# A convolution-and-attention kernel on one core: the first pass hands an eighth of its taps to GpSimd and keeps sums in PSUM, the last pass reorders ScalarE and VectorE steps and is written out without a loop

## What is computed

```
# layer 0: grouped 3x3 convolution with stride 2 (2 channels in, 1 out, 256 groups), gates, upsampling
xd  = conv(x, w_down, stride 2, padding 1, 256 groups)     # 8 x 256 x 64 x 64: 18 taps for each output
labels = kmeans(xd[0]);  gate = sigmoid(gaussian_mixture(means of xd by label))
y   = bilinear_up_x2(repeat(gate * xd + xd, 2) * w_up) + x
# layer 1: linear attention over the 64 lowest cosine frequencies of y
xp  = y @ P   (P: 16384 positions x 64 frequencies);  q, k, v from xp;  out = y + gamma * (...)
```

## Time and profile before

| | us |
|---|---|
| median of three runs | 3655.98 |
| the profiled execution: its own time | 3661.4 |
| the profiled execution: its span | 3659.6 |
| busy in the span: TensorE / VectorE / ScalarE / GpSimd | 3128.9 / 2957.6 / 1880.3 / 637.2 |
| granted TensorE clock, mean | 0.935 of full |

### The profile page before, as it was taken

One profiled execution on the slowest core, in us unless ns is written; L12 is line 12 of the kernel. 1 busy time (PEld: TensorE's weight loads), 2 busy tenths in 40 slices (PEclk: granted clock), 3 DMA queues, 4 the chain that ended last, 5 costly groups with the idle time before them and its releaser, 6 DMA issues. The chain is left out here.

```text
span 3659.6 us, 66212 instructions
## 1 busy us (share of the span) xinstructions
PE 3128.9 (85%) x23398; PEld 2253.8 (62%) x23398; DVE 2957.6 (81%) x3454; ACT 1880.3 (51%) x4327; POOL 637.2 (17%) x325
## 2 busy tenths in 40 slices
PE   7998999999899958995867888889788888888876
PEld 3554545455454526652446877878687787878776
DVE  5999999999999982204556979888897988979877
ACT  4554555555455524241316565655656566565654
POOL 0000000000000000000003333333333333333333
PEclk9999999999999979597978999999999999999999
DMA  6665566556655525252035988988888898888997
GB/s 266 256 248 212 219 257 255 222 212 251 257 233 212 238 114 204 110 217 65 0 132 212 338 331 333 351 317 337 327 326 333 328 347 331 335 326 329 345 346 287
DMA packets 190940, 947.58 MB, mean 259 GB/s; under 512 B 13505, under 2 KB 13633, under 8 KB 170626
## 3 DMA queue, kind: packets, MB, share of 16 engines
q1 hardware_dynamic: 181378, 909.48, 64.3%
q0 software_dynamic: 9216, 33.56, 2.3%
HBM read 638.90 MB, written 301.99 MB: 257 GB/s over the span
## 5 line engine op out<-in xcount | busy, mean ns | idle before, releaser
L190 DVE SCALAR_TENSOR_TENSOR first_acc<-first_x,first_wd,first_acc 128x1024 f32<-128x1024 f32 (+1 forms) x1088 | 1297.9, 1272 | 58.0 <-ACT first_acc L215 45.2
L1290 PE MATMUL second_o<-second_right,second_left 128*128 128x128 f32 x8192 | 1101.0, 285 | 175.2 <-POOL second_left L1074 98.7
L1290 PEld LDWEIGHTS second_o<-second_right,second_left 128*128 128x128 f32 x8192 | 1016.8, 199 | 229.7 <-issue 217.9
L1534 DVE SCALAR_TENSOR_TENSOR second_x<-second_o,second_shift,second_x 128x512 f32<-128x512 f32 x1024 | 732.9, 737 | 233.1 <-PE second_o L1290 231.5
L1074 POOL TENSOR_TENSOR second_left<-second_mid_copy,second_coef_rep 64x1024 f32<-64x1024 f32 x256 | 602.5, 2353 | 1684.5 <-ACT second_mid_copy L1397 1677.4
L219 ACT ACTIVATE first_xT<-first_tp 128x512 f32<-128x512 f32 x1024 | 609.3, 598 | 536.1 <-PE first_tp L245 535.6
L245 PE MATMUL first_tp<-all_const,first_x 128*128 128x128 f32 x4096 | 680.5, 291 | 75.3 <-issue 40.8
L245 PEld LDWEIGHTS first_tp<-all_const,first_x 128*128 128x128 f32 x4096 | 442.3, 143 | 458.7 <-issue 446.3
L257 PE MATMUL first_freq<-first_xT,first_p 128*64 128x256 f32 x4096 | 669.2, 408 | 17.9 <-ACT first_xT L219 8.2
L1376 ACT ACTIVATE second_mid<-second_dd,all_inter 128x128 f32<-128x128 f32 x1024 | 327.1, 390 | 388.1 <-DVE second_mid L1515 384.9
L257 PEld LDWEIGHTS first_freq<-first_xT,first_p 128*64 128x64 f32 x4096 | 210.9, 136 | 194.7 <-issue 178.9
(11 more groups left out here) (233 smaller groups left out, 2005.5 us busy)
## 6 DMA issues: line engine op xcount, KB each, us to landing
second_x<-in_x SPq DMA_DIRECT2D x256, 1024.0 KB, 10.2
out<-second_x SPq DMA_DIRECT2D x256, 1024.0 KB, 6.4
first_x<-in_x SPq DMA_DIRECT2D x48, 4224.0 KB, 25.3
first_x<-in_x SPq DMA_DIRECT2D x16, 4096.0 KB, 14.9
gather_d<-downsampled SPq DMA_DIRECT2D x24, 2048.0 KB, 12.4
downsampled<-first_acc POOLq DMA_DIRECT2D x64, 512.0 KB, 11.5
second_dd<-downsampled SPq DMA_DIRECT2D x64, 512.0 KB, 11.0
first_p<-in_p_cols SPq DMA_DIRECT2D x1, 4096.0 KB
```

Source lines behind the costliest of these rows:

```text
L190: nc.vector.scalar_tensor_tensor(out=acc[c][:, :, left:], in0=tap_window(xt[c], (s, dh, dw), OUT1), scalar=wd[:, t, k:k + 1], in1=acc[c][: ...
L1290: last = nc.tensor.matmul(ob[n][:, r, :], left[a][:, r, n, :], right[a][:, r, :], start=True, stop=True)
L1534: nc.vector.scalar_tensor_tensor(out=xt[i][:, n // S, n % S, rows, :], in0=ob[n][:, :, :], scalar=shift[:, n:n + 1], in1=xt[i][:, n // S, ...
```

## The change

First pass:

- The taps are in another order: those with dw = -1, which leave out the leftmost column, stand between dw = 0 and dw = 1, so that neither the first nor the last is one of them.
- VectorE keeps its running sums of the 17 taps in PSUM (`partial`, two tensors of 128x1024): the first tap reads `acc`, the last writes it. Chunks 0 and 1 go as before. Then come chunk 2 in two halves of 8 rows and the upper half of chunk 3, in turn, in instructions of 128x512.
- GpSimd makes the lower half of chunk 3 (an eighth of the image): for each tap a multiplication into `product` and an addition into `acc[3]`, 34 instructions of 128x512, each waiting for the one before.
- PSUM room comes from the transposes, which have two banks in place of four, and from `sum_ps`, which moves into unused columns of `freq_ps`. A transpose waits for the copy of the quad before the last.
- ScalarE's first product is made in two halves of 128x512, before the copies of quads 0 and 1, 16 and 17, 32 and 33, and for chunk 3 34 and 35.
- The stores go from GpSimd's queue to SyncE's, between the loads: store of chunk c, load of chunk c of the next image. Nothing waits for a store to land but the next first product in that buffer.
- VectorE, ScalarE and TensorE run loops of eight images, two rounds, in place of eight rounds of two; GpSimd's 16 images are written out.

Last pass: `copy` stands ahead of both halves of `weight`; `frequencies` goes from behind add 1 to behind add 3; the semaphores of loads and stores are split by t, so that the store of half t waits for that half's last add only; all eight images are written out.

```diff
-TAPS = [(s, dh, dw) for dw in (0, 1) for dh in (-1, 0, 1) for s in range(S)] + \
-       [(s, dh, -1) for dh in (-1, 0, 1) for s in range(S)]
+TAPS = [(s, dh, dw) for dw in (0, -1, 1) for dh in (-1, 0, 1) for s in range(S)]
+TP_BANKS = 2
+UNROLL1 = 4
+POOL_CHUNK = 3
+FIRST_TAPS = [0, QUADS, 2 * QUADS, 2 * QUADS + 2]
+STEPS = [TAPS_LEFT, TAPS_LEFT, 2 * TAPS_LEFT, 2 * TAPS_LEFT]
...
+        sum_ps = [bank[:, S * P:S * P + S * UV] for bank in freq_ps]
+        product = sc.sb("product", [P, OUT1 // 2, WD])
+        partial = [sc.ps(f"partial{i}", [P, OUT1, WD]) for i in range(2)]
...
+                def store(i, c):
+                    sp.wait_ge(tapped[c], i * STEPS[c] + STEPS[c] + FREE)
+                    if c == POOL_CHUNK:
+                        sp.wait_ge(upper_tapped, i * TAPS_LEFT + TAPS_LEFT + FREE)
+                    sp.dma_start(...acc[c]...).then_inc(stored[c], 16)
+                with sp.Fori(0, B * T - 1) as i:
+                    for c in range(CH1):
+                        store(i, c)
+                        load(i + 1, c)
...
+                c, rows = POOL_CHUNK, slice(OUT1 // 2, OUT1)
+                for i in range(B * T):
+                    pool.wait_ge(started, i * CH1 + c + 1)
+                    for n, (s, dh, dw) in enumerate(TAPS[1:]):
+                        nc.gpsimd.tensor_scalar(product[:, :, left:], tap_window(...), wd[...], None, ALU.mult)
+                        pool.wait_ge(tapped[c], done + 2 * n + 1)
+                        nc.gpsimd.tensor_tensor(acc[c][:, rows, left:], acc[c][:, rows, left:],
+                                                product[:, :, left:], ALU.add)
...
+                with dve.Fori(0, B // UNROLL1) as r:
+                        for n in range(TAPS_LEFT):
+                            for c in (0, 1):
+                                tap(t, c, n, slice(0, OUT1), partial[c]).then_inc(tapped[c], 1)
+                        c, half = 2, OUT1 // 2
+                        for n in range(TAPS_LEFT):
+                            for h in range(2):
+                                tap(t, c, n, slice(h * half, (h + 1) * half), partial[0])
+                            tap(t, POOL_CHUNK, n, slice(0, half), partial[1]).then_inc(upper_tapped, 1)
...
-            with eng.Fori(0, B - 1) as b:
+            for b in range(B - 1):
...
+                    for t in range(T):
+                        if u % 2 == 1:
+                            store(b, m, t)
+                        if u % 2 == 1 and (more or m + AHEAD < CH2):
+                            load_image(b, m + AHEAD, t)
...
-                    ahead = u % 2 == 1 and (more or m + 2 < CH2)
-                    if ahead:
-                        weight(b, m + 2, 0)
                     if more or u < UNITS - 1:
                         copy(b, u + 1)
-                    if ahead:
+                    if u % 2 == 1 and (more or m + 2 < CH2):
+                        weight(b, m + 2, 0)
                         weight(b, m + 2, 1)
...
-                        if n == 1 and u % 2 == 0 and (more or m + 1 < CH2):
-                            frequencies(b, m + 1)
                         if n == 2 and u % 2 == 0 and (more or m + 1 < CH2):
                             interpolate(b, m + 1)
+                        if n == 3 and u % 2 == 0 and (more or m + 1 < CH2):
+                            frequencies(b, m + 1)
```

More of the change, by code:

```diff
@@ L143, in load @@
                     sp.wait_ge(pe_read[c], i + FREE)
-                    sp.wait_ge(chunk_free[c], i + FREE)
                     above = 1 if c == 0 else 0
@@ L172, in _ @@
                 dve.wait_ge(top_zero, 1)
[L173 to L184, removed]
-                                    else:
[L187 to L196, removed]
@@ new lines, in _, with tap @@
+                start_free(dve, [*tapped[:3], upper_tapped])
+                def tap(t, c, n, rows, mine):
+                    s, dh, dw = TAPS[1 + n]
+                    left = 1 if dw < 0 else 0
+                    row0, count = rows.start, rows.stop - rows.start
+                    before = acc[c] if n == 0 else mine
+                    after = acc[c] if n == TAPS_LEFT - 1 else mine
+                    return nc.vector.scalar_tensor_tensor(
+                        out=after[:, rows, left:], in0=tap_window(xt[c], (s, dh, dw), count, row0),
+                        scalar=wd[:, t, weight_of(s, dh, dw)], in1=before[:, rows, left:],
+                        op0=ALU.mult, op1=ALU.add)
@@ L232, in _ @@
                 pe.wait_ge(top_zero, 1)
-                with pe.Fori(0, B) as b:
-                    for t in range(T):
-                        i = b * T + t
+                with pe.Fori(0, B // UNROLL1) as r:
+                    for n_image in range(UNROLL1 * T):
+                        t, i = n_image % T, r * UNROLL1 * T + n_image
                         def transpose(q):
@@ L274, in _ @@
                         for s in range(S):
-                            last = nc.tensor.matmul(sum_ps[:, s * UV:(s + 1) * UV], halves[:, s * P:(s + 1) * P], fold,
+                            last = nc.tensor.matmul(sum_ps[t][:, s * UV:(s + 1) * UV], halves[:, s * P:(s + 1) * P], fold,
                                                     start=True, stop=True)
@@ L1034, in second_pass @@
         p_in = sc.sem("p_in")
-        x_in = [sc.sem(f"x_in{i}") for i in range(XBUF)]
-        y_out = [sc.sem(f"y_out{i}") for i in range(XBUF)]
+        x_in = [[sc.sem(f"x_in{i}_{t}") for t in range(T)] for i in range(XBUF)]
+        y_out = [[sc.sem(f"y_out{i}_{t}") for t in range(T)] for i in range(XBUF)]
         dd_in = [sc.sem(f"dd_in{i}") for i in range(DSLOTS)]
@@ L1123, in prologue @@
                     for m in range(AHEAD):
-                        load_image(0, m, free=False)
+                        for t in range(T):
+                            load_image(0, m, t, free=False)
                     for i in range(XBUF):
-                        sp.sem_inc(y_out[i], Y_LEAD)
+                        for t in range(T):
+                            sp.sem_inc(y_out[i][t], Y_LEAD)
                 def step(b, u, more):
```

130 lines of the change are left out of this document (83 added, 47 removed).

## The result

The kernel after takes 3577.05 us (median of four, 3571.49 to 3578.22) against 3657.2 for the kernel before: 0.9779 of it, with a 95% interval of 0.9764 to 0.9795. That is 80 us faster where 106 were forecast, and inside the range. The profiled execution has a span of 3569.7 us; it is the quickest of the four, so the differences read from its trace add up to a little more than 80 us.

What follows compares the result with a forecast made beforehand. VectorE's taps were taken to bound the first pass, a 12.64 us chain through VectorE, ScalarE, GpSimd and TensorE the last. 3661.4 - 28 (first pass) - 77 (last pass) = 3556, with the median 5.4 lower: 3551 us; range 3492 to 3620.

Steps and rivals of the forecast that it cites:

- Taps, sums in PSUM: First pass, VectorE: 0.65 us a 512 tap, 73.7 us in sum; reading or writing PSUM costs nothing.
- rival 1: First pass: sums in PSUM cost 0.065 us more a tap, so it gains nothing; 3596 us, chance 0.13.
- Waits of the first taps beside GpSimd: First pass: three first taps with two SBUF inputs each wait 0.6 us for GpSimd, 1.8 us an image.
- GpSimd: at the edge of its cover: First pass: 34 GpSimd instructions at 1.3 us, 44 us, end under VectorE's end; cover gone at 1.57 us each.
- The chain over chunk 3's load: First pass: load, TensorE's quads and VectorE's taps take 160.4 us for two images, 80.2 each, the longest.
- The stores' end: End of first pass: some 3 us gained because the last two stores don't wait for each other.
- `zt` behind add 3: Last pass, VectorE: `zt` leaves the chain and, with GpSimd idle, takes 0.67 us in place of 1.56.
- "`copy` ahead of `weight`: 2.46 us out of the chain": Last pass, ScalarE: the first half of the weighting no longer stands ahead of the copy, 2.46 us off the chain.
- the ring on ScalarE: Last pass: next chain, bank 0 through `zt`'s transpose, copies, both weighting halves and next copy to bank 0, 11.63 us.
- The DMA bound of 12.0 us a pair: Last pass: 4.46 MB a pair at 372 GB/s take 12.0 us, the longest; 0.64 us gained a pair.
- rival 2: Last pass held by loads: at 350 GB/s in the mean a pair needs 12.7 us; 3590 us, chance 0.13.
- The loop: Last pass: writing out the images saves 3 us an image, bounds 0 and -4.

Runs made afterwards that it cites:

- moving the wait: ScalarE's first product of chunk 3 at quads 38 and 39 in place of 34 and 35, on the kernel after with ScalarE's old order: 3473.15 us.
- the run with the old order: The kernel after with ScalarE's last-pass order of before (first half of the weighting, copy, second half): 3514.49 us, 0.9597 of before.
- a version where TensorE is the bound: ScalarE's old order and chunk 3's first product at quad 38 (3473.15 us); writing out its first pass on VectorE, ScalarE and TensorE gave 3464.72 us.

## Why the prediction came out as it did

The forecast was right in direction and range, and 26 us too low. That it came so near is in part luck: up to the last pass the trace gained 41 us where 28 were put, and in the last pass 47 where 77 were, so two misses of opposite sign partly cancel. Step by step:

- **Taps, sums in PSUM: right.** 0.65 us a short tap were reckoned, 0.66 to 0.67 measured. The durations grew (799 ns where 742 were put), but the distance between starts did not, so rival 1 fell: the first pass gained, and the 62 more cycles that the prediction took from the Trainium skill ("VectorE: DVE Perf Modes", section on the TRN2 errata) do not show in these distances.
- **Waits of the first taps beside GpSimd:** 1.8 us an image were taken. The groups give a short first tap 41.6/48 = 0.87 us, 0.2 more than the others, so 0.6 for three. Oversized.
- **GpSimd: at the edge of its cover.** 1.3 us an instruction were taken and 1.57 called the edge. It is busy for 805.92/16 = 50.4 us an image, and with the gaps between its instructions its part takes 52 to 55 us by its list, 1.57 each in the mean. In every other image, the ones from which the next wait for chunk 3 follows, it ends 0.3 us behind VectorE; in the others some 7 us behind, which holds chunk 3's load back, but no wait for that load follows. That it cost nothing to speak of is luck: 1.3 us each, as put, would have left it some 8 us more. The addition was right by columns (1.34); the multiplication took 1.65 where the estimate from the Trainium skill ("GPSIMD Engine Reference", section 3.1) had 0.44, and the measurement decides.
- **The chain over chunk 3's load: right.** 80.2 us an image were reckoned and (1323.7 - 47.8)/16 = 79.7 measured, each link came within 1.2 us, and moving the wait took 34 us off the first pass.
- **The stores' end: undersized.** 3 us were put for it; 8.6 of the 40.8 us lie between the last tap and the first instruction of the next pass on VectorE (22.2 us before, 13.6 after).
- **`zt` behind add 3: right**, and worth more than the whole forecast of the last pass (84 to 89 us, against 77).
- **"`copy` ahead of `weight`: 2.46 us out of the chain": this is the step that failed.** It was out of that chain, but the move of `zt` alone had already brought the chain to 11.4 us a pair, under the 11.63 of the ring on ScalarE that the new order puts in its place, so there was nothing left to gain. And the ring was priced from rows of units where TensorE was at full clock and GpSimd undisturbed: there it took 11.6, in the last image 13.7. The step should have been made against the kernel with the other edit in, not against before. It cost 63 us.
- **The DMA bound of 12.0 us a pair: the rate was right, the bound on each pair wrong.** Pairs ran at 11.4, which asks for 4.46/11.4 = 391 GB/s. The window of seven such pairs in the run with the old order:

```profile
2131.40:2211.20 79.80, 69.42 (x531) 61.43 (x530) 72.97 (x94) 49.88 (x145) 32.07 (x14) 0.98 0.99 372
```

  372 GB/s at a share of 0.99 was the right ceiling. That is 29.7 MB where seven pairs use 31.2. But loads run three chunks ahead, and this stretch lived on what slower ones had put by; over images 0 to 6 it is 351. VectorE's adds never waited for a load, so rival 2 fell too, though its 3590 us were nearest to the result.
- **The loop: right** (3 us an image; 3.1 measured). The one loop start in the first pass: 5.5 reckoned; 8 measured by the medians and 10 in the traces, in a version where TensorE is the bound, as the matmuls behind it are slow as well.

In the last pass too the errors had opposite signs (pairs quicker than the 12.0 put, the copy's move a loss): without the copy's move the 77 us forecast there would have been 104.

## What to carry to other kernels

When a change holds two edits to one chain, price the second against the kernel that has the first; a wait that is already off the path can't be gained again. Work that is moved out from ahead of one copy lands ahead of the next. If that copy feeds TensorE, it is dearest where TensorE has nothing else to do: there the kernel pays for the idle time and for the slow matmuls behind it. When GpSimd computes beside VectorE, keep one of the two tensor inputs of VectorE's instructions out of SBUF; a long run of them with both in SBUF can hold up a single GpSimd instruction until the run ends. Look at the longest instruction of a group and not only at its mean.

## What the runs showed of the hardware

- GpSimd's multiplication by a column of scalars, reading every second element, took 1.65 us for 128x512, more than its addition of two tensors, 1.34.
- GpSimd and a VectorE instruction with two SBUF inputs wait for each other in both directions: a product of 2.35 us took 3.00 behind `interpolate`, and a `zt` of 0.67 took 2.17 behind that product.
- Behind VectorE taps with both inputs in SBUF and no gap between them, one GpSimd multiplication of 1.6 us lasted 50.1 to 54.4 us, eight times in one run: it ended only when the run of taps had.
- Behind a 3.4 us pause of TensorE the granted clock stood at its lower level (0.50 of full from 3412.7 to 3416.0 us), and eight matmuls took 1.91 us in place of 1.06; the last image's mean granted clock was 0.87 with the new order's pauses and 0.92 with the old order.
